# Router ranks behind the adapter's key projection, and two copies behind the row maxima

## The reference

```python
# attention on layernorm(x), 32 heads of 16, S = 128
q, k, v = split_heads(h @ Wq), split_heads(h @ Wk), split_heads(h @ Wv)
q, k = rope(q), rope(k)
w = softmax(q k^T / sqrt(16) + mask)
attn = w v + tanh(gate) * softmax(q (ctx Wk)^T / sqrt(16)) (ctx Wv)
x = x + attn @ Wo
# experts on layernorm(x), T = 4096 tokens
logits = xf @ router_w.T
topk_vals, topk_idx = top_k(logits, 2);  topk_w = softmax(topk_vals)
# rows sorted by expert, y = silu(gate) * up, both products per expert, weighted sum
```

## Time and profile before

| | |
|---|---|
| median of 3 runs | 2759.8 us (2749.01 to 2766.76) |
| profiled execution | 2745.8 us, span in the trace 2744.1 us |
| granted TensorE clock, mean | 0.848 of 2.4 GHz |
| busy: TensorE, VectorE, ScalarE, GpSimd | 2365, 1376, 1199, 855 us |
| attention phase | to about 2230 us of the span |
| a step inside the loop | 66 to 67 us mostly, single ones up to 78 us |

### The profile page before, as it was taken

One profiled execution on the slowest core, in us unless ns is written; L12 is line 12 of the kernel. 1 busy time (PEld: TensorE's weight loads), 2 busy tenths in 40 slices (PEclk: granted clock), 3 DMA queues, 4 the chain that ended last, 5 costly groups with the idle time before them and its releaser, 6 DMA issues. The chain is left out here.

```text
span 2744.1 us, 55286 instructions
## 1 busy us (share of the span) xinstructions
PE 2365.1 (86%) x18441; PEld 1716.4 (63%) x18442; DVE 1376.3 (50%) x4993; ACT 1199.3 (44%) x2132; POOL 854.6 (31%) x883
## 2 busy tenths in 40 slices
PE   4999998888788987888788888988888918999997
PEld 2776666666566765666566666766666715666664
DVE  4465555555455544555556565655565333333332
ACT  3555444444344443454345454544444214444433
POOL 2213322223222222222222222222233133444443
PEclk7998878788788888898889898888898658999999
DMA  2010000000000000010001010000001204444444
GB/s 93 23 48 27 27 27 27 26 27 27 27 27 27 27 27 7 25 43 28 10 27 36 26 41 27 27 27 27 27 23 18 40 26 97 85 84 83 82 82 67
DMA packets 69872, 106.45 MB, mean 39 GB/s; under 512 B 25024, under 2 KB 29120, under 8 KB 69120
## 3 DMA queue, kind: packets, MB, share of 16 engines
q0 software_dynamic: 24096, 37.51, 7.9%
q1 hardware_dynamic: 45536, 65.69, 7.8%
HBM read 67.51 MB, written 35.65 MB: 38 GB/s over the span
## 5 line engine op out<-in xcount | busy, mean ns | idle before, releaser
L1089 PE MATMUL av<-vv,pr 128*128 128x17 f32 x4096 | 617.8, 287 | 6.0 <-issue 5.7
L1089 PEld LDWEIGHTS av<-vv,pr 128*128 128x128 f32 x4096 | 609.6, 227 | 19.9 <-issue 5.9
L519 ACT ACTIVATE pr<-st 128x512 f32<-128x512 f32 x512 | 305.0, 596 | 588.9 <-PE st L1075 444.7
L699 DVE TENSOR_REDUCE mx<-md 128x4 f32<-128x512 f32 x256 | 176.7, 690 | 343.8 <-remote 223.8
L1043 PE MATMUL md<-kk,qz 128*128 128x128 f16 x2048 | 212.4, 252 | 149.3 <-DVE mx L699 92.6
L1407 PE MATMUL y<-w1s,hgT 128*128 x1704 | 280.3, 315 | 4.7 <-ACT hgT L1321 4.7
L417 POOL DMA_INDIRECT lists<-row,posi x256 | 249.0, 973 | 86.2 <-issue 86.2
L1043 PEld LDWEIGHTS md<-kk,qz 128*128 128x128 f16 x2048 | 154.6, 114 | 182.0 <-issue 129.3
L702 DVE CUSTOM_DVE_ANT_0 md<-md,msk 128x128 f32<-128x128 f32 x1024 | 264.9, 321 | 0.0
L403 POOL TENSOR_TENSOR avs<-avs,rc 128x512 f32<-128x512 f32 x32 | 34.6, 1083 | 658.3 <-DVE rc L734 658.3
L1066 PE MATMUL st<-qz,kk 128*128 128x256 f16 x1024 | 211.9, 291 | 30.0 <-issue 22.4
(11 more groups left out here) (198 smaller groups left out, 3850.8 us busy)
## 6 DMA issues: line engine op xcount, KB each, us to landing
wst<-in_w SPq DMA_DIRECT2D x32, 352.0 KB, 3.6
cin<-in_ctx SPq DMA_DIRECT2D x32, 256.0 KB, 4.0
xin<-in_x SPq DMA_DIRECT2D x32, 256.0 KB, 3.8
xres<-in_x SPq DMA_DIRECT2D x32, 256.0 KB, 3.4
out<-x SPq DMA_DIRECT2D x32, 256.0 KB, 2.1
h_pairs<-ohs SPq DMA_DIRECT2D x32, 256.0 KB
lists<-row,posi POOLq DMA_INDIRECT x256
msk<-in_mask SPq DMA_DIRECT2D x32, 64.0 KB, 3.2
```

The source lines that it names most:

```text
L519: act.activation(pr[:, path, :, :], st[path][:, :, :], ACT.Exp).then_inc(p_ex.sem, 1)
L699: dve.tensor_reduce(mx[:, 1, 4 * g:4 * g + 4], sm[1][:, :, :], AX.X, ALU.max).then_inc(s_ad.sem, 1)
L1089: i = pe.matmul(av[g // 2 % 2][:, h % 8, path, :], pr[:, path, j, :], vv[:, n.par, path, h, :], start=True, stop=True)
```

## The change

`places(c)` moves from unit 3 to unit 5, behind `ak(n)`, and writes to `ma0` instead of `md1`; it waits for the context's eviction from that bank, and `stack(n, 0)`, the bank's next writer, waits for the counts. `out_project` no longer waits for the counts. On VectorE `router_counts(c)` moves behind `residual(d)`, `router_weights(c)` behind `ak_low(n)`. `values_out(b, 2)` moves from before `maxima(n, 3)` to behind `maxima(n, 5)`, and `values_out(b, 3)` from before `maxima(n, 7)` into `neg_max`, ahead of the wait for the transposes.

```diff
--- before.py
+++ after.py
@@ -703,7 +703,7 @@
                                              ALU.add, ALU.max, mx[:, 0, h:h + 1])
             i.then_inc(s_own.sem, 1)
 
-        def neg_max(n):
+        def neg_max(n, b=None):
 
             dve.wait_ge(s_own.sem, s_own.at(n))
             dve.wait_ge(s_ad.sem, s_ad.at(n))
@@ -719,6 +719,8 @@
             dve.tensor_tensor(mr[:, :, :], mr[:, :, :], p3[1], ALU.subtract).then_inc(m_part.sem, 1)
             dve.wait_ge(m_part.sem, m_part.at(n, 4))
             dve.tensor_copy(p3[2], mr[:, :, :]).then_inc(mp3.sem, 1)
+            if b:
+                values_out(b, 3)
             dve.wait_ge(mp_t.sem, mp_t.at(n))
             dve.tensor_copy(mT[:, :, :], m_bank()[0:3 * NH]).then_inc(m_T.sem, 1)
 
@@ -812,9 +814,9 @@
         def router_counts(n):
 
             dve.wait_ge(f_p.sem, f_p.at(n))
-            dve.tensor_tensor(pos[:, :], md[1][:, 0:NE], count[:, :], ALU.add).then_inc(f_c.sem, 1)
+            dve.tensor_tensor(pos[:, :], ma[0][:, 0:NE], count[:, :], ALU.add).then_inc(f_c.sem, 1)
             dve.wait_ge(f_c.sem, f_c.at(n))
-            dve.tensor_tensor(count[:, :], md[1][:, NE:2 * NE], count[:, :], ALU.add).then_inc(f_cnt.sem, 1)
+            dve.tensor_tensor(count[:, :], ma[0][:, NE:2 * NE], count[:, :], ALU.add).then_inc(f_cnt.sem, 1)
 
         def router_weights(n):
 
@@ -857,18 +859,20 @@
                 rotate_q(n)
             if c:
                 router_top(c)
-                router_counts(c)
             if n:
                 rotate_k(n)
-            if c:
-                router_weights(c)
             values_out(b, 0)
             if d:
                 residual(d)
+            if c:
+                router_counts(c)
+            if d:
                 norm_h(d)
                 h_low(d)
             if n:
                 ak_low(n)
+            if c:
+                router_weights(c)
             values_out(b, 1)
             if d:
                 router_logits(d)
@@ -879,16 +883,15 @@
             if m:
                 norm_x(m)
             if n:
-                maxima(n, 1)
-                maxima(n, 2)
+                for g in range(1, 6):
+                    maxima(n, g)
             values_out(b, 2)
             if n:
-                for g in range(3, 7):
+                for g in range(6, 8):
                     maxima(n, g)
-            values_out(b, 3)
-            if n:
-                maxima(n, 7)
-                neg_max(n)
+                neg_max(n, b)
+            else:
+                values_out(b, 3)
 
         def first(n):
             rotate_q(n)
@@ -1025,6 +1028,7 @@
                 pe.wait_ge(q_lo.sem, q_lo.at(n))
                 pe.wait_ge(k_lo.sem, k_lo.at(n))
                 pe.wait_ge(ak_lo.sem, ak_lo.at(n))
+                pe.wait_ge(f_cnt.sem, f_cnt.at(n.shift(-3)))
             if g >= 2:
                 pe.wait_ge(stk_o.sem, stk_o.at(n, g - 1))
             turn_pairs(qs, ma[g % 2], 0, 2 * g, 2)
@@ -1097,8 +1101,6 @@
 
         def out_project(n):
             pe.wait_ge(o_T.sem, o_T.at(n))
-            pe.wait_ge(f_cnt.sem, f_cnt.at(n.shift(-1)))
-            pe.wait_ge(f_c.sem, f_c.at(n.shift(-1)))
             project(md[1], oT, wo).then_inc(o_p.sem, 1)
 
         def h_turn(n):
@@ -1110,11 +1112,14 @@
             pe.wait_ge(h_T.sem, h_T.at(n))
             project(md[1], hT, rw, NE).then_inc(r_p.sem, 1)
 
-        def places(n):
+        def places(n, ctx_batch=None):
 
             pe.wait_ge(r_sel.sem, r_sel.at(n))
-            pe.matmul(md[1][:, 0:NE], tri[:, :], sel[:, :], start=True, stop=True)
-            pe.matmul(md[1][:, NE:2 * NE], ones[:, :], sel[:, :], start=True, stop=True).then_inc(f_p.sem, 1)
+            pe.wait_ge(f_cnt.sem, f_cnt.at(n.shift(-1)))
+            if ctx_batch:
+                pe.wait_ge(c_T.sem, c_T.at(ctx_batch))
+            pe.matmul(ma[0][:, 0:NE], tri[:, :], sel[:, :], start=True, stop=True)
+            pe.matmul(ma[0][:, NE:2 * NE], ones[:, :], sel[:, :], start=True, stop=True).then_inc(f_p.sem, 1)
 
         def step(b, c, d, n, m):
             for u in range(2 * GROUPS):
@@ -1126,12 +1131,12 @@
                     ctx_turn(n)
                 if u == 2 and d:
                     out_turn(d)
-                if u == 3 and c:
-                    places(c)
                 if u == 4 and d:
                     out_project(d)
                 if u == 5 and n:
                     ak(n)
+                if u == 5 and c:
+                    places(c, n)
                 if u == 7 and d:
                     h_turn(d)
                 if u == 8 and d:
```

## The result

The changed kernel takes **2628.7 us** (median of 4 runs, 2623.47 to 2629.4). The kernel before, run beside it, takes 2760.09 us (4 runs, 2749.01 to 2766.76). The ratio is 0.9524, 95% interval 0.949 to 0.9557: 131 us less. The profiled executions differ by 117 us (2745.8 and 2628.64).

The account below looks back on a forecast made before the run. TensorE was taken to bound the kernel, losing time to waits and low clock. 17 × 3.3 + 12 × 4.0 = 104 us, less 9, gives 95; 2745.8 − 95 = 2651, plus 14 is 2664 us, range 2605 to 2725.

Parts of the forecast that it names:

- The wait for `sel`: TensorE's first rank matmul: 74.4 us in 30 waits go; gain 3.3 us in kind A, 4.0 in kind B.
- kind A: 17 of 29 steps: `sel` wait 2.25 us, projection 4.44 us; forecast gain 3.3 us each.
- kind B: 12 of 29 steps, behind the loop's jump: `sel` wait 3.03 us, projection 3.57 us; forecast gain 4.0 us each.
- The new idle before the projection: TensorE waiting for `oT`: idle of 0.6 to 1.0 us, taken to leave the clock at 2.4 GHz.
- Rival 2: Clock not won back before the projection: 39 us lost, 15 more in the tail, 2718 us; chance 0.20.
- The small exposed parts: Weights, ranks and a slightly longer low-clock tail: 0.3 us a step, 9 us in all taken off the gain.
- Counts ahead of norm_h: VectorE before h's transposes: h_low ends at 1502.9, transposes due at 1503.3, 0.4 us of cover, cost nothing.
- The weights: VectorE behind ak_low: block takes 2.1 us against 2.19 us of idle time, 0 to 0.1 us exposed.
- Rival 3: Weights in the new place make scores(0) wait on TensorE: 26 us slower, 2786 us; chance 0.06.
- The octets: VectorE's octet copies three and four: maxima(3) starts 1.4 us earlier, but maxima(4) follows the scatter; gain 0.
- rival 1: Octets help too: maxima(4) 1.4 us earlier, 41 us more, 2623 us, down to 2600 with clock held; chance 0.13.
- The wall: Before maxima(4) on VectorE: its start follows GpSimd's last list scatter, not the scores, after 5.85 us idle.

Follow-up runs that it names:

- experiment 3: Kernel before with nine unread 128 x 512 matmuls ahead of the rank matmuls' wait for `sel`: 2673.87 us, ratio 0.971.
- experiment 7: Changed kernel with `router_weights(c)` right behind `router_counts(c)`, ahead of norm_h, instead of behind ak_low: 2775.1 us, ratio 1.0047.
- experiments 1 and 2: 1: changed kernel with both octet copies in their old places, 2633.7 us (0.9571); 2: kernel before with only those copies moved, 2740.89 us (0.9966).
- Experiment 12: Changed kernel with GpSimd's scatters in four separate pairs and the octet copies in their old places, on chip 3: 2550.91 us, ratio 0.9289.
- Experiments 5 and 6: Changed kernel with its eight scatters moved: 5, in four separate pairs, 2383.02 us (0.8585); 6, in one block ahead of `x_low`, 2710.52 us (0.9824).
- the control: Changed kernel with three tiny GpSimd additions between pairs of scatters, all pairs in a row behind `x_low`, on chip 0: 2314.57 us, ratio 0.9226.
- experiment 4: Changed kernel with 32 unread 128 x 240 matmuls ahead of scores(5), in the tail: 2669.97 us, ratio 0.971.
- experiment 8: Changed kernel with scatters in four separate pairs plus 32 unread matmuls ahead of scores(5): 2438.7 us, ratio 0.8817.

## Why the prediction came out as it did

The time was 2628.7 where 2664 was forecast, within the range 2605 to 2725, and by the forecast's own case; a step lost 3.7 us (68.35 to 64.61), with 3.5 forecast. The miss of 35 us has two parts. The profiled gap was 117 us and not 95; and the 14 us by which the median of before lay above its profiled run had no counterpart after (2628.7 and 2628.64).

- **The wait for `sel`.** It went, `oT` is what is late next, and the projection starts 0.05 us behind it: as forecast. By the two kinds of step the forecast has the projection start 2.29 us earlier in the mean and take 1.33 less. Measured, it starts 2.9 us earlier (17.33 to 14.40 us after mT) and takes 1.2 less (3.98 to 2.76 in the mean). So the earlier start is the term that was mis-sized, by 0.6 us a step: the step of kind A that I worked through had its unit-3 scores and values still at 2.4 GHz, 1.9 us from the ranks to the projection; in ten of the fifteen steps inside the loop that look like it by the time of the ranks, the trace of before has 3.5 us there, and 3.9 to 4.5 for the projection. One step stood for all. Nor do the two kinds add up: 17 waits of 2.25 us and 12 of 3.03 are 74.6 us, not the 68.4 of the table, and three of the twelve steps of kind B wait only 1.0 to 1.5 us. What was missed is clock, and clock is the larger share of the gain in the head by TensorE's busy time (2.23 us, against 1.72 of idle time) and by the times of experiment 3; by the head of its trace alone it would be the smaller (1.74 of 3.97).
- **The new idle before the projection.** Forecast 0.6 to 1.0 us without loss of clock; measured 0.73 to 0.77 us, window 1.00, and the projection takes 2.76 us in all 29 steps. Rival 2 did not come.
- **The small exposed parts.** 0.3 us a step, 9 in all, were taken off; the tail shows 0.2, 6 us in all. The 22 us by which the profiled gap was undersized are about 10 in the heads, 3 here, 2 in the last step (6 us for 3.6), and 6 outside the steps, for which nothing was forecast.
- **Counts ahead of norm_h.** h_low ends at 1550.51, the transposes start at 1551.20 without a wait. The cover was there.
- **The weights.** The block takes 2.2 us, from `gap` (1552.84) to the last `tok` (1555.07), with 2.1 forecast, and is covered. Both long instructions lost their length when no GpSimd instruction stood beside them, which is what the Trainium skill (SBUF — State Buffer, "Who interferes with whom") says of the port pair that the two engines share; the trace agrees, 1.14 to 0.16 and 2.08 to 0.17 us; that the cast to `posi`, which reads one tensor, was in a two-port mode, no row shows. (`w2nd` had been long in every one of these steps of before, `posi` only in 7 of 29; in the others it took 0.17, so the forecast's 1.9 us for it held in a quarter of the steps.) Rival 3, weights that block TensorE, did not come at this place; experiment 7 has it at another, 146 us slower.
- **The octets.** Gain 0 was nearly right for this kernel (11 us alone), by the reason given: VectorE is early and waits longer (experiments 1 and 2). What I missed is that the copies can cost a lot behind that wall. Experiment 12 shows 168 us for them once the long wait is broken up on such a chip; both halves of rival 1, the earlier maxima and the clock held longer, are seen there. Without any late signals, on chip 0, the old octets leave a tail as short as the moved ones do on chip 1 (medians 22.2 and 22.6).
- **The wall.** Its place was named by its coincidence with the last scatter, and that held in the changed kernel. What it is, the prediction left unsaid. Experiments 5 and 6 tie it to eight scatters in a row (but for the three small additions, above); the control on chip 0 shows that scatters as dense need not bring it. There maxima(4) starts soon after its scores end; on chip 1, and in the runs of the result, VectorE and ACT go on only near the block's end, 5 us and more after the matmuls that they wait for (6.6 and 6.4 us in the rows after). That TensorE's signal is what is late is the reading that fits this; no run shows it apart from other readings. Chip 3 has no trace of the block: it is counted with chip 1 by its time for the kernel before and by the 0.80 us before maxima(1). Each chip was used in one or two groups of runs, so that it is the chip and not something else of the group that differs is not shown, and why stays open.
- **What it took to be right.** The forecast counted the two levels of the clock as a cost beside each wait. Without that it would have been 2.3 us a step, 66 us. There was luck in one place: that the tail would stay as it was rested on the coincidence of maxima(4) with a late scatter, whose cause was not known. On chip 0, where that does not hold, the change gains 7.7% by the control, and the forecast range ends at 5.6% (2605 us).

## What to carry to other kernels

Ask of every wait what clock the work behind it runs at, and take that from many steps, not from one: here the table of waits had 74.4 us for the wait, and the heads of the steps lost 111. A part of a change that measures as nearly nothing may be hidden by a larger wait; try it again once that wait is gone, since the copies that gave 11 us here gave 168 with the scatters spread, on the chips with the wall. The best kernel found for those chips is the changed one with the scatters in four pairs apart (2383.0 us, ratio 0.8585); where the wall is absent, spreading the scatters made the kernel before 1.7% slower, and the changed kernel with the scatters together is the fastest measured (2314.6 us).

## What was not expected of the hardware

- **VectorE and ACT go on late beside eight scatters in a row, on some chips.** maxima(4) starts 8.5 to 10.1 us after the first scatter in nearly every step of the kernel before and the changed one, and of experiments 1 to 3 on chip 1, and 2.98 us in the control on chip 0. ACT's exponentials are late with it. The kernel before takes 2760.09, 2752.33, 2764.17 and 2749.17 us in four groups of runs and 2532.72 in the group on chip 0, for the same program.
- **TensorE slows beside them too.** The added matmuls of experiment 4 paused 127 times, 88.4 us in all, with nothing in the trace to wait for; with the scatters spread (experiment 8) they paused twice, 2.2 us in all.
- **A short idle can cost several times its length.** 0.73 to 0.77 us ahead of the projection left the clock at 1.00; 1.22 us (experiment 7) and 1.15 with 0.54 close behind (experiment 12) were followed by 13.6 us at 0.53 and 0.51. Not every such idle drops the clock: experiment 7 has other steps with the same 1.22 us, a clock of 1.00 behind it and a head 6 to 8 us shorter, so a step whose clock fell lost about five times its idle time.
